# Expert tiles as three products of split operands, and the persistent keys' transposed scores in four column groups

## The reference

```
x = x + attn_a(norm(x))   # rotations and a gated scan over time, 6 heads of 64
x = x + ffn(norm(x))      # 8 experts, hidden size 176, the best 2 for each token
x = x + attn_b(norm(x))   # 16 heads of 16, window of 128, the first 16 keys always seen
x = x + ffn(norm(x))      # the same expert weights again
```

## Time and profile before

| | us |
|---|---|
| median of 3 runs | 783.53 |
| lowest, highest run | 776.94, 786.41 |
| span of the profiled execution, first to last instruction | 780.9 |
| PE busy | 645.8 (83%) |
| DVE busy | 466.2 (60%) |
| POOL busy | 342.0 (44%) |
| ACT busy | 296.7 (38%) |

### The profile page before, as it was taken

One profiled execution on the slowest core, in us unless ns is written; L12 is line 12 of the kernel. 1 busy time (PEld: TensorE's weight loads), 2 busy tenths in 40 slices (PEclk: granted clock), 3 DMA queues, 4 the chain that ended last, 5 costly groups with the idle time before them and its releaser, 6 DMA issues. The chain is left out here.

```text
span 780.9 us, 14537 instructions
## 1 busy us (share of the span) xinstructions
PE 645.8 (83%) x4707; PEld 503.9 (65%) x4707; DVE 466.2 (60%) x1226; ACT 296.7 (38%) x567; POOL 342.0 (44%) x406
## 2 busy tenths in 40 slices
PE   0889999994569999924689999999899868999960
PEld 0668787773447677713578788878778645777740
DVE  6894859787626434463665767876852454644423
ACT  1363444351014444432344545545433322444430
POOL 4304051616413767743513434445545470653335
PEclk9989999895858999956669999999965555999995
DMA  8699400151122633275432340431307211443329
GB/s 268 214 351 350 149 1 8 37 116 44 43 65 85 195 104 97 85 233 88 81 56 30 83 81 12 76 89 50 80 16 201 100 58 44 134 140 97 102 74 315
DMA packets 68317, 86.92 MB, mean 111 GB/s; under 512 B 8909, under 2 KB 62802, under 8 KB 67380
## 3 DMA queue, kind: packets, MB, share of 16 engines
q1 hardware_dynamic: 61428, 67.80, 32.4%
q0 software_dynamic: 6816, 18.19, 6.5%
HBM read 35.13 MB, written 39.06 MB: 95 GB/s over the span
## 5 line engine op out<-in xcount | busy, mean ns | idle before, releaser
L1292 POOL DMA_INDIRECT back<-f_yout,f_target x78 | 76.7, 983 | 113.7 <-ACT f_yout L1399 103.0
L1334 PE MATMUL bank<-f_wgu,f_xt 128*128 x312 | 113.7, 489 | 3.4 <-ACT f_xt L1384 3.3
L1181 POOL DMA_INDIRECT xs<-xn,f_slots x64 | 65.0, 1016 | 56.7 <-ACT xn L1172 41.1
L1439 DVE TENSOR_TENSOR f_hid<-f_act_g,bank 128x176 f32<-128x176 f32 x78 | 26.3, 338 | 104.5 <-ACT f_act_g L1391 100.4
L2066 POOL TENSOR_SCALAR_AFFINE_SELECT b_prob<-b_prob 128x512 f32<-128x512 f32 x60 | 38.1, 635 | 112.7 <-ACT b_prob L2307 112.4
L2307 ACT ACTIVATE b_prob<-bank 128x1024 f32<-128x1024 f32 x60 | 61.4, 1023 | 55.8 <-PE bank L2146 55.5
L1356 PE MATMUL bank<-f_wd,f_hT 88*128 x312 | 81.4, 385 | 0.0
L1334 PEld LDWEIGHTS bank<-f_wgu,f_xt 128*128 128x128 f32 x312 | 59.1, 199 | 31.3 <-issue 9.9
L2376 DVE COPY_PREDICATED bank<-b_later,bank 128x512 f32<-128x512 int32 x60 | 41.6, 694 | 47.0 <-PE bank L2116 42.4
L1356 PEld LDWEIGHTS bank<-f_wd,f_hT 88*128 88x128 f32 x312 | 54.2, 193 | 4.8
L1399 ACT ACTIVATE f_yout<-bank,f_share 128x256 f32<-128x256 f32 x78 | 36.9, 473 | 39.9 <-PE bank L1356 38.9
(11 more groups left out here) (313 smaller groups left out, 1519.4 us busy)
## 6 DMA issues: line engine op xcount, KB each, us to landing
xs<-xTf SPq DMA_DIRECT2D x8, 2176.0 KB, 19.3
f_xin<-xs SPq DMA_DIRECT2D x78, 136.0 KB, 2.1
f_wgu<-in_wgu SPq DMA_DIRECT2D x4, 1408.0 KB, 14.3
f_wgu<-back SPq DMA_DIRECT2D x16, 256.0 KB, 5.1
b_KS<-b_kh SPq DMA_DIRECT2D x32, 128.0 KB, 3.9
b_QS<-b_qh SPq DMA_DIRECT2D x32, 128.0 KB, 3.9
f_back<-back SPq DMA_DIRECT2D x8, 512.0 KB, 7.5
f_wd<-in_wd SPq DMA_DIRECT2D x4, 968.0 KB
```

The source lines that it names most:

```text
L1181: pool.indirect_dma_start(m.xs, bass.IndirectOffsetOnAxis(m.slots[:, g, c, i:i + 1], 0), xn[:, g * TPC + i], None)\
L1292: pool.indirect_dma_start(m.back, bass.IndirectOffsetOnAxis(target[:, g % AR:g % AR + 1], 0), yout[:, g % YB], None, bounds_check=2 * 2 * ...
L1334: mm = pe.matmul(psG[:, g % 2, 0:2 * FH], xt[:, g % 2, k * P:(k + 1) * P], m.gu[:, k, bass.ds(e, 2 * FH)], start=k == 0, stop=k == KD - 1)
```

## The change

**Experts.** Both products of a tile become three F32R products each: `xth`, `xtl` with `guh`, `gul`, and `hTh`, `hTl` with `wdh`, `wdl`. ACT makes the high half of x and of hid (`x_high`, `hid_high`) and DVE the low one (`x_low`, `hid_low`). `psX` holds two transposed tiles now, `xin` is transposed two tiles ahead, and the down product comes three steps late instead of two. The tile buffers lie where `QS` and `KS` lie later, so that the pads can't be written before the last tile is sent.

**Weights.** For turn 0 the recurrence splits them in quarters: ACT copies, POOL subtracts for gate and up (2 x 704 elements a quarter; two quarters in each of the chunks 1 and 2) and DVE for down (in chunk 3). For turn 1 the attention does it in eighths in its periods 15 to 19, on ACT and DVE; the loads of gate and up move to periods 5 and 7.

**Persistent keys.** `KPT` has 32 columns for each slot, and slot s writes the PSUM rows 32 * (s % 4) and on, as a plain fp32 product.

```diff
@@ experts, tensor @@
-                    pe.wait_ge(xt_done, g + 1)
+                    pe.wait_ge(xtl_done, g + 1)
 ...
                     for k in range(KD):
-                        mm = pe.matmul(psG[:, g % 2, 0:2 * FH], xt[:, g % 2, k * P:(k + 1) * P], m.gu[:, k, bass.ds(e, 2 * FH)],
-                                       start=k == 0, stop=k == KD - 1)
+                        for xx, w in ((xth, guh), (xth, gul), (xtl, guh)):
+                            mm = pe.matmul(psG[:, g % 2, 0:2 * FH], xx[:, g % 2, k * P:(k + 1) * P], w[:, k, bass.ds(e, 2 * FH)],
+                                           start=n == 0, stop=n == 3 * KD - 1)
 ...
+                x_transposed(1)
                 for s in range(STEPS):
                     if s < G:
                         gate_up(s)
 ...
+                    if s + 2 < G:
+                        x_transposed(s + 2)
+                    if 0 <= s - DOWN_AFTER < G:
+                        down(s - DOWN_AFTER)
                     if 0 <= s - 1 < G:
                         hid_transposed(s - 1)
-                    if s + 1 < G:
-                        x_transposed(s + 1)
-                    if 0 <= s - 2 < G:
-                        down(s - 2)
@@ experts, vector @@
+                def x_low(j):
+                    g = tiles(j)
+                    dve.wait_ge(xth_done, g + 1)
+                    dve.tensor_tensor(xtl[:, g % 2], psX[:, g % 2, 0:D], xth[:, g % 2].bitcast(F32),
+                                      ALU.subtract).then_inc(xtl_done, 1)
 ...
                     if s < G:
                         hidden(s)
-                    if 0 <= s - 1 < G:
-                        hidden_out(s - 1)
+                    if s + 2 < G:
+                        x_low(s + 2)
                     if s < G:
                         aim(s)
+                    if 0 <= s - 1 < G:
+                        hid_low(s - 1)
@@ Routed @@
+    def up_low_part(self, eng, turn, q):
+        part = self.eighth(q) if turn else self.quarter(q)
+        eng.tensor_tensor(self.gu[:, :, part].bitcast(F32R), self.gu[:, :, part], self.gu_high[turn][:, :, part].bitcast(F32),
+                          ALU.subtract).then_inc(self.up_low, 1)
@@ recurrence, gpsimd @@
                     if it + 1 < NCH:
                         decays(it + 1)
+                    if 0 < it < NCH - 1:
+                        for q in (2 * it - 2, 2 * it - 1):
+                            pool.wait_ge(m.up_high, q + 1)
+                            m.up_low_part(pool, 0, q)
@@ attention, lead_pool @@
-            padded(pool)
+            for i in range(4):
+                pad(pool, i)
+            padded(pool, 1)
             for p in range(1, FIRST_PAIRS + 1):
                 pair_first(pool, p)
                 pair_deviation(pool, p - 1)
 ...
             pair_deviation(pool, FIRST_PAIRS)
+            pool.wait_ge(u_off, FIRST_PAIRS + 1)
+            for i in range(4, 12):
+                pad(pool, i)
+            padded(pool, RING // 2)
@@ attention, transposed_persist @@
-                        mm = pe.matmul(psT[:, 0, g * P:(g + 1) * P], KPT[:, s], QS[:, s, ring(b)],
-                                       start=b > 1 and s % NQUAD == 0, stop=s % NQUAD == NQUAD - 1, skip_group_check=True)
+                        mm = pe.matmul(psT[32 * i:32 * (i + 1), 0, g * P:(g + 1) * P], KPT[:, s].bitcast(F32),
+                                       QS[:, s, ring(b)].bitcast(F32), start=b > 1, stop=True, skip_group_check=True)
@@ attention, vector, in a period's step @@
+                        if (n, u) in UP_PARTS:
+                            part = UP_PARTS.index((n, u))
+                            dve.wait_ge(m.up_high, LOW_PARTS[0] + part + 1)
+                            m.up_low_part(dve, 1, part)
```

More of the change, by code:

```diff
@@ L80, in build @@
         x = sb("x_tok", [P, T // P * D])
-        xTh = sb("xTh", [P, KD, PAD + T], F32R)
-        xTl = sb("xTl", [P, KD, PAD + T], F32R)
+        xTboth = sb("xTboth", [P, 2 * KD * (PAD + T)], F32R)
+        xTh, xTl = (xTboth[:, i * KD * (PAD + T):(i + 1) * KD * (PAD + T)].rearrange("p (k c) -> p k c", k=KD) for i in range(2))
         xTf = sb("xTf", [P, KD, 2, CH])
@@ L840, in _ @@
                         group.payload(xn)
+                    if not ahead:
+                        for q in (0, 1):
+                            dve.wait_ge(m.dn_high, q + 1)
+                            m.down_low_part(dve, 0, q)
                     if ahead:
@@ L1298, in _ @@
                         pool_scatter(pool, m, xn, turn, g3, *SENDS[j - SEND_AT])
-                    if not last and j >= LEAD_FROM and j % 2 == 0 and (j - LEAD_FROM) // 2 < lead["pads"]:
-                        lead["pad"](pool, (j - LEAD_FROM) // 2)
                 def first_rows(g):
@@ L1308, in _ @@
                 else:
+                    for r in range(YB):
+                        pool.wait_ge(y_out[r], 16 * uses(tile_no(turn, G), r, YB))
                     lead["pool"](pool)
@@ L1453, in _ @@
                 group, table = Routing(dve, m, turn, g3), Table(dve, m, turn, 1)
-                group.take(psZ)
+                group.take(logits)
+                x_low(0)
+                x_low(1)
                 group.compare()
@@ L1567, in attention @@
         later = sb("later", [P, P], I32)
+        vbuf = sb("V", [P, RAW])
+        with ExitStack() as tiles_too:
+            routing.take_tile_buffers(nc, tiles_too)
         QS = sb("QS", [P, SLOTS, RING * P], F32R)
@@ L2000, in lead_dve @@
             pair_low(dve, 2)
-        lead = dict(load_weights=load_weights, pad=pad, pads=len(pads), sp=lead_sp, pool=lead_pool, pe=lead_pe, act=lead_act, dve=lead_dve)
+        lead = dict(load_weights=load_weights, sp=lead_sp, pool=lead_pool, pe=lead_pe, act=lead_act, dve=lead_dve)
     def periods():
@@ L2369, in _ @@
                             act_tanh(act, m, xn, 1, RATIOS[n, u])
+                        if (n, u) in UP_PARTS:
+                            part = m.eighth(UP_PARTS.index((n, u)))
+                            act.wait_ge(m.w_in, 16 * KD * 2)
+                            act.wait_ge(q_ready, NHC)
+                            act.wait_ge(lat_ready, NHC)
+                            act.activation(m.gu_high[1][:, :, part], m.gu[:, :, part], ACT.Copy).then_inc(m.up_high, 1)
+                        if (n, u) in DOWN_PARTS:
+                            part = m.eighth(DOWN_PARTS.index((n, u)))
+                            act.wait_ge(m.d_in, 32 * 2)
+                            act.wait_ge(t_ready, quad(NB - 1, NQUAD))
+                            act.activation(m.wd_high[1][:, :, part], m.wd[:, :, part], ACT.Copy).then_inc(m.dn_high, 1)
             @block.vector
```

182 lines of the change are left out of this document (123 added, 59 removed).

## The result

The changed kernel takes **799.73 us** (median of 4 runs, 791.2 to 809.38); the kernel before took 780.82 beside it (776.94 to 786.41). The ratio is 1.021, with a 95% interval of 1.013 to 1.029: the changed kernel is slower, by about 2%, at the edge of what was called no change. The run of 809.38 was a slow one, at a mean clock of 0.825, and is left out of the ratio. The forecast was 787, its range 765 to 806. The time is inside the range, but 13 us above the forecast. The stages show that all four parts of the sum (recurrence, turns, lead, periods) came out worse than forecast.

The account below looks back on a forecast made before the run. DVE was taken to bound the recurrence, PE the attention. Turns -9.2, recurrence +9.4, lead +9, column groups -8, eighths +2 gave +3.2 on a 780.9 span, 784.1; with 2.6 between span and runs, 787 us, range 765 to 806.

Parts of the forecast that it names:

- turns: Both expert turns: -4.1 us each, and -1.0 for a stall that already exists, -9.2 in all (bounds -26 to +25).
- periods: Attention periods: -8 us from the column groups and +2 from DVE's eighths, a forecast of -6.
- the tile's products: Expert tiles: 0.12 us per narrow product of 256 columns, so a tile takes 2.15 us on PE instead of 2.48.
- the taps held by POOL: Recurrence: POOL's subtractions hold DVE's taps, line 729 comes 4.7 us late, +9.4 for two chunks (0 to +14).
- the end of the recurrence: DVE's four subtractions of `wd` fall where it waits for PE and the stage's end: 0 us.
- all go on 0.8 us behind POOL's eighth pad: Lead: POOL ends its pads at 375.0 us and all engines go on at some 375.8; the lead's term is +9.
- the ring of loads: Expert loop: 4.06 us for two tiles, 2.03 a tile, just below 2.15; routing +1.5 and late landings +3 a turn.
- ring of loads decides: Rival, expert loop: landings of about 3.0 us make a tile 2.48, nothing is saved, 810 us; chance 0.10.
- tile 17: Expert turns: its load waits for POOL's eight sends of the last group, a PE stall of 4.7 us.
- the eighths: Attention periods 18 and 19: DVE's subtractions of turn 1's weights meet the tail, +2 us (0 to +18).
- the column groups: Attention, persistent keys: eight products take 0.49 us instead of 1.04, 0.55 saved 15 times, -8 us (0 to -9).
- two rivals on the clock: Attention: PE's clock falls earlier, 814 us, chance 0.07; or it stays up, 768 us, chance 0.08.

Follow-up runs that it names:

- run 1: Changed kernel with the four low-half subtractions for gate and up moved from POOL to DVE, in the recurrence's last chunk: 786.69 us, ratio 1.013.
- run 5: Changed kernel with low halves of gate and up on DVE, eight pads in periods 0 and 1, and early last-group sends together: 773.27 us, ratio 0.984.
- run 9: Changed kernel with run 5's three edits, a ring of six loaded tiles, and SP's seven loads spread behind every second tile: 750.14 us, ratio 0.965.
- run 10: Run 9's kernel with turn 1's loads of gate and up in periods 11 and 13 instead of 5 and 7: 753.42 us, ratio 0.966.
- run 11: Run 9's kernel with the lead's four remaining pads behind the deviations of pairs 0 and 1 instead of at its head: 752.42 us, ratio 0.965.
- 12: Run 9's kernel with DVE's last four eighths of `wd` moved to the head of its list in turn 1: 750.18 us, ratio 0.960.
- 2: Changed kernel with the lead's last eight pads moved behind the wait of all engines, into periods 0 and 1: 786.63 us, ratio 1.010.
- run 6: Kernel before the change, with only the persistent keys' column groups added: 766.07 us, ratio 0.975.
- 3: Changed kernel with the eight sends of the last group's rows after tiles 0 to 5 instead of 3 to 10: 788.45 us, ratio 1.015.
- run 4: Changed kernel with the persistent keys' operand put back to one F32R operand of 128 columns: 806.92 us, ratio 1.030.
- run 7: Changed kernel with DVE's sixteen subtractions of turn 1's weights cut to 4 columns each: 790.33 us, ratio 1.007.
- run 8: Changed kernel with a ring of six loaded tiles instead of four: 782.84 us, ratio 1.002.

## Why the prediction was right and where it was not

As a whole it held: 799.73 us lies in the range of 765 to 806. But the forecast for the span was +3.2 us and the measured change +16.3, and all of its four parts erred to the same side: recurrence 2.1, turns 3.8, lead 4.4, periods 3.4.

**Right: the tile's products.** 2.11 us where nothing else holds PE, against 2.15 from 0.12 for each 256 columns. With six loads in the ring it is the period of all later tiles.

**Right: the taps held by POOL.** The copy of three elements was the right row to argue from the earlier trace rows. 4.7 us a chunk was forecast. The chunk takes 4.8 more up to DVE's addition to x (149.53), of which 3.7 are the taps and 1.1 the longer carry copy, and both chunks together take 8.7 more; run 1, without POOL's subtractions, gives 7.5 of it back. The page "SBUF — State Buffer" of the Trainium skill, section "Who interferes with whom", was used twice, and the traces agree where they can: a cast beside pads takes 1.91 against 0.21, and an addition with two SBUF inputs beside a pad 0.67 against 0.69, free of it. Its exclusive lock is what these rows look like. That line 729 itself would be held no row shows, since POOL was done before it began.

**Mis-sized: the end of the recurrence, put at nothing.** From DVE's last norm but one to the first gate and up it takes 38.36 instead of 35.63, 2.7 more. The subtractions of `wd`, the only part that the prediction weighed there, are at most 0.7 of it, and by a way that it did not see. Before and in the changed kernel:

```profile
217.04 0.96 POOL L1181 DMA_INDIRECT xs<-xn,f_slots  x1 [0.30 <-issue]
...
221.94 3.55 PE L994 MATMUL bank<-f_wr_raw,xTf 128*128 128x8 f32 x16 [4.99 <-PEq L180]
```
```profile
225.70 3.16 DVE L968 TENSOR_TENSOR f_wd<-f_wd,xTboth 88x1408 fp32r<-88x1408 f32 x2
226.42 1.02 ACT L171 ACTIVATE xTf<-bank 128x1024 f32<-128x1024 f32 x1 [13.56 <-PE bank L162]
226.47 1.69 POOL L1251 DMA_INDIRECT xs<-xn,f_slots  x1 [0.30 <-issue]
...
232.11 3.55 PE L1064 MATMUL bank<-f_wr_raw,xTf 128*128 128x8 f32 x16 [5.72 <-PEq L180]
```

All engines go on 3.95 us behind POOL's last send in both kernels, and in every run in which DVE isn't late (3.94 to 3.96). In the runs in which DVE ends late (1, 5 and 9 to 12) they go on 1.49 behind DVE, so that DVE, which ends 3.25 before, was not the last in the changed kernel: its cover held. But beside its subtraction POOL's last send takes 1.69 instead of 0.96. Another 0.9 is the head of the tiles: from there to the first gate and up it is 5.50 instead of 4.63, since two tiles are transposed and a low half subtracted first. The remaining 1.1 lie ahead of DVE's last addition to x. There PE takes, among others, 7.83 instead of 7.11 for the same 24 products (line 434, before 432) at a lower clock (0.68 against 0.81 in the windows 209 to 218 and 200 to 209).

**Wrong: that all go on 0.8 us behind POOL's eighth pad.** The release at 363.27 was put down to SP, and that reading may well be right: in the kernel before and in the runs 2, 6, 9, 10 and 12 all go on 0.7 behind SP's last issue and 4.84 to 4.86 behind POOL's last operation, in the runs 5 and 11 at 4.25 behind POOL and 1.0 behind SP. So POOL alone would have let them go at 4.25 or less. What failed is the slack that was read from it: POOL's end was taken to need no time of its own, and 0.8 us was put behind the eighth pad. Where POOL is clearly last, in the changed kernel and in the runs 1, 3, 4, 7 and 8, all go on 4.49 behind it. That is 3.7 of the 4.4 by which the lead missed (+13.4 instead of +9). The eight pads take 14.8 instead of 14.4, and POOL's delay by the first four, forecast as 2.2, is 2.5.

**Mis-sized: the ring of loads.** The forecast had 2.03 us a tile for it, just below PE's 2.15, and put 4.5 us a turn on late landings and routing. The ring itself held the loop: 0.19 a tile in the later half of turn 0, 0.24 in turn 1, more beside the sends. The later half shows where the 4.06 for two tiles was short: from a tile's transposes to the issue of the load two tiles on it is 1.94 (1.83 forecast without hand-overs), and from the issue to its transposes 2.6 in turn 0 and 2.8 in turn 1, where 2.1 of landing and some hand-overs were put: 4.6 and 4.7 in all. Run 8 prices the ring at 5.7 and 7.2 us a turn even with a larger stall at tile 17, run 9 against run 5 at 12.4 a turn with the spread loads. The rival "ring of loads decides" was the right mechanism, but it was tied to landings of 2.35 and more; with a median of 2.1 a slack of 0.12 us was already none.

**Right in size, partly by luck: tile 17.** Forecast 4.7; 4.98 in turn 1, and the clock falls behind it. But the distance from the last send to the transpose, 4.24, was read from tile 16's transpose; tile 17's comes 5.5 or 5.6 behind the send's start in turn 1 of both kernels (691.32 to 696.91, 706.62 to 712.11). PE also asked for it later than forecast, at 39.6 from the start of the turn instead of 38.0, and the two errors nearly cancel. In turn 0 tile 17 waits only 0.74, behind the 3.00 of tile 16. That stall is SP's seven loads ahead of a tile's load, of which the prediction says nothing: they cost 1.04 before, 3.00 now, and 0.95 with six loads in the ring (run 8), where the tiles have more slack. That turn 0 came within 0.5 of its forecast is therefore partly luck; turn 1 missed its own by 3.3.

**Right: the eighths.** +2 was forecast, run 7 gives 2.65 in the tail. The tail as a whole is 3.3 longer (36.56 instead of 33.22), and most of the rest is the longer head of the tiles, 5.22 instead of 4.63, as in turn 0.

**Mis-sized, and wrong on the clock: the column groups.** The eight products take 0.65 instead of 1.11 (0.49 was forecast), and a period 0.37 less, not 0.55: 5.5 us in all instead of 8. No run shows what of the missing 0.18 is a drain of TensorE. The Trainium skill, page "TensorEngine Tiling (Array Packing)", section "Key Properties", names such a drain, without a figure. The clock was taken as unchanged "between 440 and 600", and it isn't. It falls at 532 for 10 us and comes back, and again at 577 and later. The two rivals on the clock were both partly true, one early dip and no long stretch. Against the kernel before they nearly cancel; against the old operand in the changed kernel they are some 7 us to the good (run 4). In the kernel before with groups alone, only the good part is there, and that makes it 2.5% faster.

**Open.** Why the clock dips in period 8. It does in all runs with groups and the rest of the change (1, 2, 3, 5, 7 to 12), but not in 4 and 6. PE's largest gap ahead of it (0.83) is the same in run 6, which has no dip. Run 7 excludes DVE's eighths, run 10 the early loads, and the start of the periods, between 354 and 389 us, doesn't matter either.

## What to carry to other kernels

When PE's work in a loop gets shorter, work out again every ring and every queue whose slack was counted in the old period, and give a ring more buffers than its sum asks for: here buffers for two more tiles were worth 13 us in the two turns. Work that moves to the end of a block costs its length plus the exit of the engine that it makes the last one, and the exits differ: 0.3 us behind DVE or ACT at the end of the periods, 4.5 behind POOL at the end of the lead. Look up in several runs how far behind each engine's last operation the others go on, before you name who held them: the same distance in two runs doesn't show it, if another engine's distance is the same too. And cut a change into its parts: one part here was worth 2.5% alone, while the whole was a loss of 2%.

## What the runs showed of the hardware that was not expected

- How far the exit from a block lies behind its last operation depends on the engine: 4.49 us behind POOL's last memset (lead, six profiles), 3.94 to 3.96 behind POOL's last indirect DMA (recurrence, eight profiles), 1.49 behind DVE's last subtraction (recurrence, six profiles), 0.32 behind DVE's at the end of the periods, and 0.30 and 0.51 behind ACT's last copy there (runs 12 and 7).
- POOL's last indirect DMA of the recurrence took 1.69 us beside a DVE subtraction with both inputs in SBUF, and 0.96 without one.
- Two back-to-back POOL subtractions of 1408 elements (6.36 us) held the first of DVE's tensor-scalar taps for 6.12; it did not get in between them. In run 11 a tensor-scalar of two elements took 1.64 beside a pad (0.17 otherwise).
- Sixteen records of plain fp32 products in four column groups took 0.65 us at full clock and 1.08 at half.
- TensorE's granted clock can come back after 7 to 10 us at half, in the middle of dense work, as well as stay down nearly all the way from 571 to 661, as before: the same products in another form made the difference.
